# Keys' side of a linear attention cut into 64 units, moved ahead and spread out

## What is computed

```
x = layernorm(x + state_space(x))            # W_in, conv, scan over 16 states, gate, W_out
x = layernorm(x + xattn(x, ctx))
x = layernorm(x + experts(x))                # router, top 2 of 4, rank 16

# xattn, per batch, 128 channels, n = 1024, 8 heads of 64
qh, kh, vh = Wq q, Wk k, Wv k                # k = ctx
qh = softmax(qh, over the 64) * 64 ** -0.5
kh = softmax(kh, over n)
context = kh vh^T ;  out = context^T qh
out = Wo out + bo ;  out = out / |out| * g * sqrt(128)
```

## Time and profile before

| | |
|---|---|
| time, median of 3 runs (lowest, highest) | 3033.13 us (3032.32, 3034.54) |
| the profiled execution: time, span | 3033.12 us, 3031.0 us |
| TensorE (PE) busy | 2745.5 us, 91% of the span |
| VectorE (DVE) busy | 2552.6 us, 84% |
| GpSimd (POOL) busy | 1926.4 us, 64% |
| ScalarE (ACT) busy | 1693.4 us, 56% |
| DMA, mean | 93 GB/s |
| mean granted clock of TensorE | 0.959 of full speed |

### The profile page before, as it was taken

One profiled execution on the slowest core, in us unless ns is written; L12 is line 12 of the kernel. 1 busy time (PEld: TensorE's weight loads), 2 busy tenths in 40 slices (PEclk: granted clock), 3 DMA queues, 4 the chain that ended last, 5 costly groups with the idle time before them and its releaser, 6 DMA issues.

```text
span 3031.0 us, 35275 instructions
## 1 busy us (share of the span) xinstructions
PE 2745.5 (91%) x11120; PEld 1568.1 (52%) x11120; DVE 2552.6 (84%) x3522; ACT 1693.4 (56%) x2846; POOL 1926.4 (64%) x884
## 2 busy tenths in 40 slices
PE   8968899999989999998999888898878999999996
PEld 4535555555555555555555444555444555555553
DVE  2359999999999999999999999999936787777775
ACT  2347566565665657556565565665605555555553
POOL 1159897888969889797898987988802222222221
PEclk9989899999999999999999998898889999999998
DMA  5432333424343344334333322322121111111110
GB/s 171 135 100 80 99 98 106 138 87 131 87 155 106 93 128 126 107 94 143 115 94 98 94 86 85 119 85 77 42 70 70 62 55 55 62 62 54 56 62 21
DMA packets 132876, 281.32 MB, mean 93 GB/s; under 512 B 12528, under 2 KB 12656, under 8 KB 132224
## 3 DMA queue, kind: packets, MB, share of 16 engines
q1 hardware_dynamic: 132736, 279.59, 29.6%
HBM read 245.86 MB, written 33.69 MB: 92 GB/s over the span
## 4 chain that ended last, share of the span: by engine, by line
PE 55%; DVE 31%; issue 9%; ACT 4%; POOL 1%; DMA 0%; DVEq 0%; SPq 0%; ACTq 0%; POOLq 0%
DVE arena L1216 17%; PE banks L454 15%; PE banks L478 9%; DVE arena L1232 7%; PE banks L536 7%; PE banks L629 4%; PE banks L672 4%; PE banks L585 3%; PE banks L610 3%; PE banks L491 2%; PE banks L640 2%; PE banks L600 2%; ACT banks L981 1%; DVE arena L1172 1%; PE banks L679 1%
## 5 line engine op out<-in xcount | busy, mean ns | idle before, releaser
L1142 POOL TENSOR_TENSOR arena<-arena 128x2048 f32<-128x2048 f32 x256 | 1162.3, 4540 | 78.7 <-PE banks L536 78.5
L1216 DVE TENSOR_TENSOR_SCAN arena<-banks,arena 128x512 f32<-128x512 f32 x1024 | 1185.1, 1204 | 20.0 <-POOL arena L1142 16.8
L981 ACT ACTIVATE banks<-arena,a_sb 128x508 f32<-128x508 f32 x1024 | 696.9, 684 | 735.2 <-DVE arena L1216 734.7
L454 PE MATMUL banks<-arena 128*128 128x512 f32 x2048 | 955.8, 604 | 11.6 <-DMA arena<-in_xT 8.7
L536 PEld LDWEIGHTS banks<-ident,arena 128*128 128x128 f32 x4096 | 493.5, 146 | 418.9 <-issue 197.0
L536 PE MATMUL banks<-ident,arena 128*128 128x128 f32 x4096 | 576.5, 284 | 137.3 <-DVE arena L1232 68.9
L454 PEld LDWEIGHTS banks<-arena 128*128 128x128 f32 x2048 | 374.1, 195 | 365.4 <-issue 362.2
L1232 DVE SCALAR_TENSOR_TENSOR arena<-banks,cg,arena 128x512 f32<-128x512 f32 x640 | 452.9, 738 | 71.6 <-PE banks L536 70.9
L478 PE MATMUL banks<-arena 128*128 128x512 f32 x1024 | 473.0, 601 | 3.0 <-DVE arena L1336 3.0
L1088 POOL TENSOR_TENSOR arena<-arena 128x512 f32<-128x512 f32 x240 | 306.2, 1276 | 204.1 <-ACT arena L811 201.8
L1153 POOL TENSOR_TENSOR arena<-arena 128x512 f32<-128x512 f32 x128 | 141.3, 1104 | 462.8 <-DVE arena L1382 462.8
(11 more groups left out here) (137 smaller groups left out, 2979.2 us busy)
## 6 DMA issues: line engine op xcount, KB each, us to landing
arena<-b_scratch SPq DMA_DIRECT2D x128, 512.0 KB, 5.1
arena<-in_WinX SPq DMA_DIRECT2D x128, 256.0 KB, 2.8
arena<-in_WinZ SPq DMA_DIRECT2D x128, 256.0 KB, 2.7
arena<-in_WoutT SPq DMA_DIRECT2D x32, 1024.0 KB, 5.3
u_scratch<-arena SPq DMA_DIRECT2D x64, 256.0 KB, 5.1
arena<-u_scratch SPq DMA_DIRECT2D x16, 1024.0 KB, 9.5
arena<-x_scratch SPq DMA_DIRECT2D x32, 512.0 KB, 3.5
arena<-in_xT SPq DMA_DIRECT2D x14, 1024.0 KB, 8.0
```

Of the source, the lines that this page charges most:

```text
L454: last = nc.tensor.matmul(home(kind, i), wr[w % 2][:, k, :], x[:, k, :], start=(k == 0), stop=(k == KC - 1))
L981: nc.scalar.activation(by_seq(bank(i % 2))[:, :, 1:SEQ], by_seq(dt[s % 2][:, i, :])[:, :, 1:SEQ], ACT.Exp, scale=a_sb[:, QD * q + i, n:n + ...
L1142: nc.gpsimd.tensor_tensor(hb[n % 4].rearrange("p (i t) -> p i t", i=QD), dtu, brep[pair % 3][:, n % 2:n % 2 + 1, :].broadcast_to([P, QD, G ...
L1216: nc.vector.tensor_tensor_scan(h, bank(i % 2), h, 0.0, ALU.mult, ALU.add)\
```

## The change

The keys' side becomes 64 units, v = 4k + o for batch k and block o. A unit is K (keys, two multiplications of 512 columns), a minimum on VectorE and an exponential on ScalarE, T (eight transposes), G (context, eight multiplications of 128 columns), and after the last o of a batch V (values). `wk` is stored negated, so that VectorE's minimum is the negative maximum and its extra negation goes; the factor 64 ** -0.5 is put into `ph`. The result `mt` of a batch is stored to DRAM and loaded again in slot 8 of its batch.

19 units lie in the last four quads, at the turns of `KEY_TURNS`; 45 follow in the batches, one per 3.7 slots (`SLOT`). In the last four quads the job order is `SPARE` and `LAST` instead of `ORDER`, with Z, D and O on banks 6 and 7 alone, while units use 4 and 5; ScalarE's and VectorE's parts of these jobs move with them (`act_between`, `dve_spare`). The constants and the first row of x1 are loaded in the last quad, wk, Wv and Wo in the one before the last four. The eight last output tiles go into slots 0 to 2 of batch 0 (`OUTS`). All batches are written out, with no loop.

```diff
+SPARE = "Z0 Z1 D0 Z2 D1 O0 D2 O1 O2 D3 O3 Z3 O4 O5 O6 O7".split()
+SPARE_BANK = dict(zip(SPARE, (6, 7, 6, 7, 6, 7, 6, 7, 6, 6, 7, 6, 7, 6, 6, 7)))
+SPARE_SIZES = [1, 1, 3, 3, 2, 3] * 5 + [2, 1]
+LAST = "Z0 O0 O1 O2 O3 Z1 Z2 Z3 O4 O5 O6 O7".split()
+LAST_BANK = dict(zip(LAST, (6, 7, 6, 7, 6, 7, 6, 7, 6, 7, 6, 7)))
+LAST_SIZES = [1, 1, 3, 3, 2, 3] * 4 + [1, 1, 3, 3, 2, 2, 0, 0]
...
+SPARED = NS - 4
+KEY_TURNS = [N * s + n for s in range(SPARED, NS) for n in ((0, 3, 6, 9, 12) if s + 1 < NS else (0, 3, 6, 9))]
...
+OUTS = (0, 1, 2), (3, 4, 5), (6, 7)
+SLOT = {v: 1 + 37 * (v - KUNITS) // 10 for v in range(KUNITS, UNITS)}
...
+        def sync_constants(sp):
+
+            sp.wait_ge(S["fin"], QD * (NS - 1))
+            for dst, name in consts2:
+                sp.dma_start(dst, a[name]).then_inc(S["p2_const"], 16)
+            sp.wait_ge(S["x1_stored"], 16 * (NG - 1))
+            sync_x1_row(sp, 0)
...
+        def pe_context(pe, k, o, dst):
+            pe.wait_ge(S["et_ok"], 2 * (OT * k + o) + 2)
+            pe.wait_ge(S["ct_loaded"], 16 * k + 16)
+            for t in range(NT):
+                last = nc.tensor.matmul(dst, cT[:, t, :], ekT[:, t, :], start=(t == 0), stop=(t == NT - 1))
+            last.then_inc(S["g_mm"], 1)
...
+        def pe_units(pe, b, t):
+
+            v = slot_unit(b, t, 6)
+            if v is not None and v % OT == OT - 1:
+                pe_values(pe, v // OT, bank(6))
+            v = slot_unit(b, t, 4)
+            if v is not None:
+                pe.wait_ge(S["g_ok"], v)
+                pe.wait_ge(S["mt_ok"], v // OT)
+                pe_context(pe, v // OT, v % OT, bank(6)[:, 0:P])
+            v = slot_unit(b, t, 2)
+            if v is not None:
+                pe_keys_turn(pe, v // OT, v % OT, bank(2), bank(3))
+            v = slot_unit(b, t, 0)
+            if v is not None:
+                pe.wait_ge(S["et_ok"], 2 * v)
+                pe_keys(pe, v // OT, v % OT, banks[1][:, :])
...
+        def dve_keys(dve, k, o, src):
+
+            v = OT * k + o
+            dve.wait_ge(S["k_mm"], v + 1)
+            after(dve, "k_exp", v - 1)
+            nc.vector.tensor_reduce(nkm[:, o % 2:o % 2 + 1], src, AX_X, ALU.min).then_inc(S["k_max"], 1)
...
+        def dve_spare(dve, s, half):
+
+            for c, at in enumerate((15, 17, 19, 22, 27, 28, 30) if s + 1 < NS else (7, 9, 10, 12, 25, 27, 29)):
+                if half == at:
+                    dve_out(dve, s, c)
+            for i, at in enumerate((12, 14, 17, 20) if s + 1 < NS else ()):
+                if half == at:
+                    dve_dt(dve, QD * (s + 1) + i)
```

644 lines of the change are left out of this document (405 added, 239 removed).

## The result

The changed kernel takes **3170.11 us** (median of 4 runs, 3167.46 to 3174.35), the kernel before 3032.99. The ratio is 1.0454 (95% interval 1.0441 to 1.0467): 4.5% **slower**, where I forecast 2987 and a gain. The profiled execution has a span of 3172.5 us; TensorE's mean granted clock is 0.947 (0.959 before).

The account below looks back on a forecast made before the run. VectorE was taken to bound the last four quads, TensorE's matmuls the batches. Terms +42 (three quads), 0 (last quad), −35 (way to batches), −53 (batches) sum to −46, so 2987 us; range 2944 to 3022.

Parts of the forecast that it names:

- Cost of one unit: One key block of one batch: 4.33 us on TensorE, sixteen narrow products taken at 1.74; one 1.21 us reduction on VectorE.
- Rival 5: Narrow products slower because load and stream do not overlap: 1.75 us more a unit, +79, 3066 us; chance 0.03.
- The last four quads: They take 19 units; VectorE's work and new waits add 14 us a quad, +42 for the first three.
- four waits: Turns 4, 9, 5 and 8 of the first three quads, from two shared banks: 10.0 us lost per quad.
- of that I let 4 stay: Of VectorE's 7.1 us idle time in a quad now, 4 us remains beside the new waits.
- My upper end, +20 a quad: Upper end for the first three quads, if no idle time is absorbed and SyncE's queue adds waits.
- The last quad, 0: Four units add 5.6 us, eight fewer filler steps at its end save 6.9; taken as 0 (−3 to +8).
- Quad 11, 0: Products for the heads' matrices and wk's negation cost 0, covered by TensorE's idle time, 4 us if not.
- The way to the batches, −35: From the last quad to the second batch: 88.0 us becomes 53, 35 less (−30 to −38).
- The batch, 41.5: Batch period as a chain of engines, 41.5 us, 3.6 less than 45.1; −53 over all batches (−30 to −75).
- rival 4: Waits before x2's transposes drop batches to 1.2 GHz: 4.3 us a batch, 65 in all, 3052 us; chance 0.05.
- rival 3: Quads clogged: the first three of the last four at +22 each, the last at +8, 3019 us; chance 0.11.

Follow-up runs that it names:

- e6_no_units: Changed kernel with all 64 units left out of quads and batches, two banks and written order kept in the last four quads; 2985.8 us.
- e9_four: Changed kernel with four units in the last quad, sixty in batches, four banks in other quads, copies, multiplication and last weights early; 3056.85 us, ratio 1.0071.
- e5_ends: Changed kernel with the third output block's residual addition and last output weights earlier; last four quads 530.9 us (17.0 less), way to first attending product 66.6 (6.5 less).
- e7b_pin_values: Changed kernel with units in slots 1, 4 and 8 of every batch and VectorE's values multiplication one slot earlier, ahead of the gates; 3065.64 us.
- e3_copy_early: Changed kernel, drifting slots kept, with ScalarE's copies of the turned keys one slot earlier, ahead of the query's exponential; 3139.74 us.

## Why the prediction was wrong

**Cost of one unit: right.** Sixteen narrow products take 1.79 us start to start (L763 at 2479.48, L748 at 2481.27), against the 1.74 that I took. That is 0.112 us each, a quarter of the 0.430 of a wide one (1.72 for four). Rival 5 is out. The Trainium skill's sustained gaps for a load and matmul pair, 81 ns at 128 columns against 131 at 512 (TensorE: Matmul & The Clock Gate, section Back-to-back issue gap), do not describe this fp32 row: here the time goes by columns.

**The last four quads: mechanism right, size off.** I said +42 for three quads: 20 for VectorE's work of the units, 30 for four waits, less 8 of idle time absorbed. In those three quads VectorE's busy time rose by 7.5, 7.9 and 7.0 us, 22.4 against my 20. Its idle time came to 21.9, 21.4 and 21.6 us, where I had 14 (10.0 for the waits and the 4 that I let stay); before it was 5.3 to 6.9. So the work was sized right and the idle time was not, and most of the +68.9 is there without units too (+54.8 in `e6_no_units`, with VectorE idle 22.5 to 23.1). The terms that failed are the 10.0 a quad for the four places and "of that I let 4 stay": what VectorE waits for before its accumulations, 27 us more in `e6_no_units`, are TensorE's transposes, and the fillers that wait for a bank stand ahead of them in TensorE's order. How the excess divides between the two terms was not tried; that one mended place of 11.7 us gave 17.0 says that a place costs more than its wait. My upper end, +20 a quad with nothing absorbed, was passed too: +22 to +23.

**The last quad, 0: right** (+1.4), and in its terms: 4.1 less without units and 5.5 more for its four units, against my 6.9 and 5.6. **Quad 11, 0, "4 us if not":** about 4.5, by the end of quad 11 at 1739 to 1743 us in the kernels with two banks in four quads and 1735 to 1738 in the others; `e9_four` has the same loads and products in quad 14, and that quad takes 7.6 more than before. Which piece of it costs this was not tried.

**The way to the batches, −35: too much.** Measured −22. Of the 13 missing, `e5_ends` gave 6.5 back: I did not ask what the second half of the last weights waits for once the constants no longer cover it. This is the question of what is late next, which I had asked in the quads only. The rest I did not take apart.

**The batch, 41.5: the step that failed.** It is the chain 25.8 + 10.4 + 5.0 = 41.2, taken as if the units lay beside it. The floor without any unit is 41.0, but that the two agree is luck: its pieces are 22.9, 11.8 and 6.2 (the rows of `e6_no_units`), the third with the experts' product at 1.2 GHz in it. With three units in good slots they are 26.9 to 27.3, 12.0 to 13.5 and 4.5 to 6.1 (`e7b_pin_values`, nearly all at full clock), so the first two are passed by 1.1 us and more even there, and in the change, from its second batch to its fourteenth, 26.0 to 37.7, 10.6 to 15.6 and 4.5 to 11.0. I took the two reductions and products that I saw on the chain away, and put none of the new ones on it. The 142 us between 628.6 (681.6 − 53) and 770.7 are, by the runs:
- 42: three units in good slots cost a batch about 3 us more than I gave it (670.7);
- 22: the multiplication queued behind the gates (692.2 − 670.7);
- 78: the slots that the drift reaches (770.7 − 692.2). Of them the key products' waits for copies that ScalarE holds behind an exponential are shown to be worth 28 (`e3_copy_early`). The rest, waits for the multiplication, products ahead of the squares and of the experts, is read from the rows and was not taken apart.

A smaller slip went the same way: I gave a batch 45/16 units, but the 45 stand in fifteen batches, three in each.

In each of these places a short instruction in an in-order queue stands ahead of or behind one that waits for another engine. I counted busy time and walked the chain of two batches; I never laid the new pieces over the eleven slots, which the list of instructions would have let me do.

**The rivals.** The clock (rival 4, 0.05) had the sign, and its mark came too: a period over 44 with the granted clock at 0.91. It is not what began the loss: in `e7b_pin_values` only slots and the place of one instruction differ in the batches, the clock is 0.98 over the stretch and the mean period 44.3. But it is a part of the price: TensorE is busy 624.5 us over the stretch of the change and 582.6 over that of `e7b_pin_values`, with the same products, 41.9 us more at the lower clock in a stretch that is 100 us longer. How much of the 41.9 the engines' chain had to wait for is not shown; `e9_four` shows 3.0 us for one batch. Clogged quads (rival 3) came true at +22 to +23 each, and with my other terms kept would have left the time at 3015. A range of 2944 to 3022 took its lower side from a gain in the batches of up to 75, while the kernel before stands only 67 above the floor of that stretch; I had no case in which the batches got worse by order.

## What to carry to other kernels

Before work is moved out of a loop, ask how far the loop stands above the time that it takes without this work at all: here 4.1 us of 45.1 a batch, 67 us in all, at the clock that this run had, while the room made for the work in the quads cost 51 and the work there 20. Small pieces spread over a loop by a formula visit every slot, so each piece has to be checked in each slot against the in-order queue of each engine it uses, above all where one engine's piece stands behind another's wait. And run the parts of a change alone: the small part (loads moved up, 3018 us) was worth 0.5%, while the whole lost 4.5%.
